# A four-block transformer kernel: the entries of its two narrow attentions reordered

## The reference

```python
x = x + _L0_xattn_ref(_layernorm(x), ctx_1024, ctx_1024, wq, bq, wk, bk, wv, bv, wo, bo)
# inside: q from the norm of x; k and v from the context
scores = einsum('bthd,bshd->bhts', q, k) / sqrt(8)
probs  = softmax(scores)
x = x + (einsum('bhts,bshd->bthd', probs, v) @ wo.T + bo)
```

## Time and profile before

| | |
|---|---|
| times of three runs | 816.60, 821.52 and 816.17 us, median 816.6 |
| profiled execution | 821.47 us, of which the span of the records is 819.8 us |
| PE | 719.1 us busy, 88% of the span |
| DVE | 517.8 us, 63% |
| ACT | 439.8 us, 54% |
| POOL | 373.7 us, 46% |
| mean granted PE clock | 0.927 |

### The profile page before, as it was taken

The page is one execution under the profiler, slowest core; times in us unless marked ns, Lnnn a source line. Parts: engine busy times, 40 slices in busy tenths (PEclk is TensorE's granted clock), DMA queues, the critical chain, the costliest instruction groups (busy, mean ns, idle before and its releaser), DMA issues. The chain is left out here.

```text
span 819.8 us, 14606 instructions
## 1 busy us (share of the span) xinstructions
PE 719.1 (88%) x4942; PEld 584.4 (71%) x4942; DVE 517.8 (63%) x1415; ACT 439.8 (54%) x1344; POOL 373.7 (46%) x375
## 2 busy tenths in 40 slices
PE   6986799999899999897679999788879999996775
PEld 3654699998688887775558788556658888884754
DVE  5797774445676666575646677758765566566554
ACT  3893334444577776563124777489734466653221
POOL 6663312112576644433112677485441488864001
PEclk9599799999999999998959999979989999998669
DMA  7000011110000000000003445000010322200000
GB/s 277 2 2 26 14 27 52 40 49 14 1 2 2 2 8 2 1 1 0 7 21 97 145 141 177 16 2 2 3 48 26 103 97 90 78 14 1 0 1 26
DMA packets 14277, 33.13 MB, mean 40 GB/s; under 512 B 1744, under 2 KB 5864, under 8 KB 13952
## 3 DMA queue, kind: packets, MB, share of 16 engines
q1 hardware_dynamic: 14208, 32.26, 12.0%
HBM read 31.63 MB, written 0.62 MB: 39 GB/s over the span
## 5 line engine op out<-in xcount | busy, mean ns | idle before, releaser
L1233 PE MATMUL banks<-input_hi,weights_in_lo 128*128 128x512 f32 x296 | 123.9, 418 | 18.4 <-PEq L1617 11.9
L1233 PE MATMUL banks<-input_lo,weights_in_hi 128*128 128x512 f32 x296 | 118.9, 402 | 0.0
L1233 PE MATMUL banks<-input_hi,weights_in_hi 128*128 128x512 f32 x296 | 118.6, 401 | 0.0
L1233 PEld LDWEIGHTS banks<-weights_out,hidden 128*128 128x128 f32 x864 | 105.6, 200 | 11.1 <-issue 8.1
L1233 PE MATMUL banks<-weights_out,hidden 128*128 128x128 f32 x864 | 106.9, 284 | 7.0 <-PEq L1561 6.3
L992 ACT ACTIVATE probabilities<-banks,neg_max 128x128 f32<-128x128 f32 x256 | 92.3, 479 | 17.5 <-DVE neg_max L1945 17.5
L1095 ACT ACTIVATE hidden<-banks,cols 128x512 f32<-128x512 f32 x80 | 54.1, 689 | 75.5 <-ACTq L1093 75.1
L703 POOL TENSOR_TENSOR rstd<-var_eps,neg_half 128x4 f32<-128x4 f32 x24 | 24.9, 1038 | 136.1 <-POOLq L702 115.2
L1233 PEld LDWEIGHTS banks<-input_hi,weights_in_lo 128*128 128x128 f32 x296 | 57.5, 194 | 32.4 <-issue 17.3
L992 ACT ACTIVATION_READ_ACCUMULATOR probabilities<-banks,neg_max 128x1 f32 x256 | 72.9, 319 | 0.0
L813 POOL TENSOR_TENSOR hidden<-hidden,scratch 128x512 f32<-128x512 f32 x48 | 62.0, 1291 | 19.4 <-ACT hidden L1114 16.8
(11 more groups left out here) (277 smaller groups left out, 1734.3 us busy)
## 6 DMA issues: line engine op xcount, KB each, us to landing
scratch<-cw_rows SPq DMA_DIRECT2D x19, 512.0 KB, 3.9
weights_out<-w_in SPq DMA_DIRECT2D x17, 256.0 KB, 2.8
weights_in<-w_in SPq DMA_DIRECT2D x8, 512.0 KB, 3.6
weights_in<-w_in SPq DMA_DIRECT2D x9, 256.0 KB, 3.0
weights_in<-w_in SPq DMA_DIRECT2D x16, 128.0 KB, 2.2
weights_out<-w_in SPq DMA_DIRECT2D x16, 128.0 KB, 2.1
wq<-w1q_in SPq DMA_DIRECT2D x1, 1024.0 KB, 4.9
wo<-w1o_in SPq DMA_DIRECT2D x1, 1024.0 KB, 7.0
```

Of the source, the lines that this page charges most:

```text
L1233: return pe.matmul(o, l, rh, start=start, stop=stop, **kw)
```

## The change

On the SP queue x is loaded in two halves: first half, square weights, context, second half, with a semaphore of its own for the second. The statistics of each half wait for their own load.

In the plain attention PE now has the order keys of half 0, transposes of half 0, keys of half 1, queries of half 0, values. The other transposes (`turn_rest`, into bank 7 and no longer bank 1) come in step 1, the second half's queries in step 2 (before: step 0). ACT copies the second half's transposes after unit 0's exponentials (`rest_state`), and DVE copies the values after the maxima of unit 1 (`first_values`) and the second half's queries after those of unit 2. ACT does one exponential of a 128x1 column before anything else.

In the pruned attention PE's keys, values and transposes of half 0 come ahead; DVE does the second sum, then the norm of half 0, the split of the keys, the statistics of half 1, and the queries. The norm of half 1 follows the maxima of unit 0 (`rest_norm`), its power on POOL follows the first batch's queries and keys; transposes, values and queries of half 1 are placed as in the plain attention. In both, `add_bias` on POOL now waits for the second half's queries.

```diff
 # SP
-            sp.dma_start(x[:, :, :], x_in).then_inc(x_loaded, 16)
+            first = SQS["wk1"][0]
+            sp.dma_start(x[:, 0:4, :], x_in[:, 0:4, :]).then_inc(x_loaded, 16)
+            sp.dma_start(sq[:, 0:first], sq_in[:, 0:first]).then_inc(sq_loaded, 16)
             sp.dma_start(ctxT[:, :], ctxT_in).then_inc(ctx_loaded, 16)
-            first = SQS["wk1"][0]
-            sp.dma_start(sq[:, 0:first], sq_in[:, 0:first]).then_inc(sq_loaded, 16)
+            sp.dma_start(x[:, 4:8, :], x_in[:, 4:8, :]).then_inc(x_rest_loaded, 16)
 # POOL, spread_queries_keys and add_bias
+                    if prune and n == 0:
+                        inverse_roots((1,))
...
+                    pool.wait_ge(queries_ready, 2 * prune + 2)
                     pool.tensor_tensor(x[:, :, :], x[:, :, :], row_b("bo2" if prune else "bo0"), ALU.add)\
 # ACT
+            def take_state(half):
+                act.wait_ge(transposed, 1)
+                act.sem_inc(transposed, -1)
+                act.activation(xnT[:, half * 512:(half + 1) * 512], bank[7 * half][:, :], ACT.Copy)\
+                    .then_inc(feat_ready, 1)
             def enter_narrow(prune):
...
+                round_keys(prune, 0)
+                if prune:
+                    round_keys(prune, 1)
+                take_state(0)
+                if not prune:
+                    round_keys(prune, 1)
...
-                    pipelined(act, [(exps, range(UNITS), 1)], UNITS, 1, st.close)
+                    pipelined(act, [(exps, range(UNITS), 1), (rest_state, (0,), 1)], UNITS, 1, st.close)
...
             act.wait_ge(cols_loaded, 16)
+            act.activation(gap_exp[:, 0:1], col("bq0"), ACT.Exp).then_inc(st.sem, st.one())
+            act.wait_ge(st.sem, st.n)
+            st.close()
 # PE, steps (the pruned list is changed alike)
-                    pipelined(pe, [(scores, range(UNITS), 0), (rest_queries, (0,), 0),
+                    pipelined(pe, [(scores, range(UNITS), 0), (turn_rest, (0,), 1), (rest_queries, (0,), 2),
                                    (values, range(1, UNITS, 2), 3), (turn, range(UNITS), 2),
 # PE, entries
-            project(w("wk0"), ctxT, 2, (0, 1), keys_projected)
-            transpose_tiles(xn)
+            project(w("wk0"), ctxT, 2, (0,), keys_projected)
+            transpose_half(0, xn, 0)
+            project(w("wk0"), ctxT, 2, (1,), keys_projected)
...
             project_tok(w("wv2"), ctxT, 4)
-            transpose_tiles(xn)
+            transpose_half(0, xn, 0)
 # DVE, steps of the pruned and of the plain attention
                     pipelined(dve, [(pad, (0,), 0), (inverse_sums, range(UNITS), 2), (maxima, range(UNITS), 0),
-                                    (rest_queries, (0,), 0), (copy_second, range(UNITS), 2),
+                                    (rest_norm, (0,), 0), (first_values, (0,), 1), (rest_queries, (0,), 2),
+                                    (copy_second, range(UNITS), 2),
...
-                                    (rest_queries, (0,), 0), (scale_out, range(1, UNITS, 2), 3),
+                                    (first_values, (0,), 1), (rest_queries, (0,), 2), (scale_out, range(1, UNITS, 2), 3),
 # DVE, entries
-            split_keys(False)
+            split_keys(False, 0)
+            split_keys(False, 1)
             copy_queries(False, 0)
-            copy_values(iv, 4, "bv0", values_copied)
...
-            for half in range(2):
-                add_sums(half)
-                norm_stats(half, x, 1e-5)
-            for half in range(2):
-                norm_apply(half, x, xn, norm_tok_ready)
-            split_keys(True)
-            copy_values(iv, 4, "bv2", values_copied)
+            add_sums(0)
+            norm_stats(0, x, 1e-5)
+            add_sums(1)
+            norm_apply(0, x, xn, norm_tok_ready)
+            split_keys(True, 0)
+            split_keys(True, 1)
+            norm_stats(1, x, 1e-5)
             copy_queries(True, 0)
```

More of the change, by code:

```diff
@@ L973, in enter_halves, with round_keys @@
                 return take
-            def enter_narrow(prune):
-                for half in range(2):
[L977 to L980, removed]
-                for half in range(2):
[L982 to L985, removed]
+            def round_keys(prune, half):
+                tokens = slice(half * 512, (half + 1) * 512)
+                act.wait_ge(keys_projected, 2 * prune + half + 1)
+                act.activation(in_hi[:, 0, tokens], bank[2 + half][:, :], ACT.Identity,
+                               bias=col("bk2" if prune else "bk0")).then_inc(keys_rounded, 1)
+            def take_state(half):
[3 more added lines that the diff above has]
+                    .then_inc(feat_ready, 1)
+            def enter_narrow(prune):
+                round_keys(prune, 0)
[4 more added lines that the diff above has]
+                    round_keys(prune, 1)
             def narrow_attention(prune):
@@ L1000, in copy_first, with rest_state @@
                         .then_inc(first_copied[prune], 1)
+                def rest_state(it, n):
+                    take_state(1)
                 if prune:
-                    pipelined(act, [(exps, range(UNITS), 1), (copy_first, range(UNITS), 2)], UNITS, 1, st.close)
+                    pipelined(act, [(exps, range(UNITS), 1), (rest_state, (0,), 1), (copy_first, range(UNITS), 2)],
+                              UNITS, 1, st.close)
                 else:
-                    pipelined(act, [(exps, range(UNITS), 1)], UNITS, 1, st.close)
+                    pipelined(act, [(exps, range(UNITS), 1), (rest_state, (0,), 1)], UNITS, 1, st.close)
             def round_heads():
@@ L1275, in narrow_attention, with turn_rest @@
             def narrow_attention(prune):
+                def turn_rest(it, n):
+                    transpose_half(1, xn, 7)
                 def rest_queries(it, n):
+                    pe.wait_ge(feat_ready, 1)
+                    pe.sem_inc(feat_ready, -1)
                     project(w("wq2" if prune else "wq0"), xnT, 6, (1,))
@@ L1891, in norm_x @@
                 for half in range(2):
+                    dve.wait_ge((x_loaded, x_rest_loaded)[half], 16)
                     norm_stats(half, x, 1e-5)
@@ L1904, in copy_queries @@
             def copy_queries(prune, half):
-                dve.wait_ge(projected, 1)
+                dve.wait_ge(projected, 3 if prune and half == 0 else 1)
                 dve.sem_inc(projected, -1)
@@ L1910, in copy_queries, with split_keys @@
                     .then_inc(queries_ready, 1)
[L1912 to L1919, removed]
+            def split_keys(prune, half):
+                tokens = slice(half * 512, (half + 1) * 512)
+                dve.wait_ge(keys_rounded, 2 * prune + half + 1)
+                dve.scalar_tensor_tensor(in_lo[:, 0, tokens], bank[2 + half][:, :],
+                                         col("bk2" if prune else "bk0"), in_hi[:, 0, tokens],
+                                         ALU.add, ALU.subtract).then_inc(keys_split, 1)
             def copy_values(dst, at, bias, done=None):
@@ L1946, in maxima, with rest_norm, first_values @@
                         .then_inc(neg_max_ready[prune], 1)
+                def rest_norm(it, n):
+                    norm_apply(1, x, xn, norm_tok_ready)
+                def first_values(it, n):
+                    copy_values(iv, 4, "bv2" if prune else "bv0", values_copied)
                 def rest_queries(it, n):
```

11 lines of the change are left out of this document (4 added, 7 removed).

## The result

| | before | after |
|---|---|---|
| median of 7 runs each, same comparison | 817.28 us (816.17 to 821.52) | 826.13 us (824.24 to 830.52) |
| ratio after / before | | 1.0107 [1.0084, 1.0131], +8.85 us |
| profiled execution / its span | 821.5 / 819.8 us | 830.5 / 828.8 us |
| plain attention ends (taken at the start of its first addition into x) | 72.84 | 77.00 (+4.16) |
| sums ahead of the pruned attention start | 521.18 | 525.02 (+3.84) |

The distance between the two profiled executions, 9.05 us, is about that of the medians, so their traces can be set side by side. 4.2 us arise in the plain attention, 3.5 in the pruned one, 1.7 behind it. The last is no effect of the change that could be told from chance: the code behind the pruned attention is the same everywhere and takes 215.8 to 218.0 us in the profiles of this document (216.0 before, 217.7 after).

What follows compares the result with a forecast made beforehand. DVE was taken as tighter in the plain attention, ACT's start as deciding the pruned one, PE's clock as third. Plain entry +1.6, plain steps +2.5 and the rest 0 gave +4.1 on median 816.6; predicted 820.5, range 813 to 826.5.

Steps and rivals of the forecast that it cites:

- rival A: Slow clock stretch comes every time, in plain steps 1 to 3: 824.8, with +1.3 in the pruned attention 826; chance 0.25.
- the forecast's own range: Whole kernel: 818 to 823.5 us, given a chance of 0.45.
- Loads: Start of kernel, loads and first norm: halving and reordering x costs nothing, bound 0 to +0.3 us.
- Table load: ACT at the start: pulling the 1.28 us table load ahead gains nothing, as ACT would have been free anyway.
- Plain entry: Plain attention's start: PE waits for the norm and works at half speed, first queries end later; +1.6 (+0.4 to +1.6).
- Plain steps: Plain attention, steps 0 to 4: DVE's order delays `turn` 0 and maxima 4, start 13.3 after scores 0; +2.5 (+0.6 to +2.5).
- DVE being the tighter engine: Plain attention running evenly, 3.11 us a unit: DVE tighter than ACT, so a late maximum delays all that follow it.
- Pruned entry: Pruned attention's start: first exponential 2.5 us earlier, then given back; taken at 0 (-1.7 to +1.3).
- the branch at half clock: Pruned entry: scores 2, queries and transposes in one half-speed chain, unit 3's exponentials at 47.1 for 545.9; +1.2, with a wait +1.3.
- Each sign that was named: Pruned attention: first exponential 2.5 us earlier against the block before, ACT idle 1 to 3 us ahead of the first `copy_first`.
- the reading of the median: Median 816.6 taken as an execution without the plain attention's slow stretch, which cost about 4.1 us; profiled execution 821.5.

Runs made afterwards that it cites:

- retimed kernel: Kernel before with pruned attention as changed, but its second half's norm, transposes, state copy, values and queries one place earlier: 815.8 us, ratio 0.9973.
- changed kernel with the old loads: The changed kernel with x loaded whole and in the old order on the SP queue: 825.2 us, ratio 1.0073 against before.
- key order alone: Kernel before with only the transposes of half 0 put between the two halves' keys in the plain entry, on PE and ACT: 818.4 us, ratio 1.0013.
- plain part alone: The whole change except the pruned attention, which stays as before: 823.3 us, ratio 1.0074 against before.
- after filled: Changed kernel plus unread extra PE matmuls ahead of the pruned scores 0 and of units 0 to 4's transposes: 824.1 us, ratio 1.0070 against before.
- steps alone: Kernel before with only the plain attention's second transposes, values' copy and second queries moved to steps 1 and 2: 822.7 us, ratio 1.0069.
- pruned part alone: Kernel before with only the pruned attention changed, on all engines: 817.2 us, ratio 1.0006.
- loads alone: Kernel before with only x loaded in halves and the new order on the SP queue: 819.2 us, ratio 1.0023.
- before, filled: Kernel before plus twelve unread PE matmuls: two ahead of pruned scores 0, one ahead of units 0 to 4's transposes in both attentions: 819.5 us, ratio 1.0011.
- with values as before: Kernel before with the pruned attention changed, but its values copied ahead of the first steps, right after the first queries: 819.7 us, ratio 1.0004.
- with the table load: The retimed kernel plus one early exponential first on ACT: 816.1 us, ratio 0.9988 against before.
- retimed, filled: The retimed kernel plus the same unread extra PE matmuls: 817.8 us, ratio 1.0000 against before.

## Why the prediction was right or wrong

The time lies in the range, and the sign was right, but it lies only 0.4 below the upper end, in a part that was added for rival A; the forecast's own range ended at 823.5. The likeliest value, 820.5, is 5.6 too low: an increase of 4.1 was worked out and 8.85 measured. 826.1 is what rival A gave, by a mechanism that the runs don't bear out. That the range holds it is in good part luck.

**Loads: the step that failed.** "Nothing (0 to +0.3)" measured +1.5 at scores 0 and +1.9 [0.4, 3.3] in the time. I took it that the same bytes ahead of the context and the cols land when they did. Before, keys waited for the last of x, context and square weights, at 6.43; now the context is that last one, at 7.57, and the second half of x (8.11 for "6.5 at the earliest") holds DVE in a norm that wanted both. Keys, which I had perhaps 0.6 earlier, start 1.1 later.

**Table load: right.** The retimed kernel is not faster with it.

**Plain entry: the mechanism right, the size +1.1 for +1.6.** The changed kernel with the old loads measures this term: the queries end at 14.09 for the 14.6 worked out at half speed and 13.03 before, and scores 0 start at 15.94 for 16.5 and 14.88. They do run at half speed, 1.79 for 1.10. That the key order alone came to 14.7 and 16.55 is a coincidence, since it has a second group of transposes ahead of the queries which the sum did not have. Loads and order together make +2.57, of which 1.5 are the loads'. The choice of half speed was right, and other kernels bear it out. Where PE stood 1.1 to 1.6 us ahead of its first transposes (after, plain part alone, key order alone, old loads, after filled), the first queries take 1.55 to 1.92 us; in all other kernels, where it ran on from the keys, 1.09 to 1.10.

**Plain steps: the chain right, its size mixed with the clock.** `turn` 0 waits for the queries' copy, and maxima 4 stand where DVE's order puts them: 3.1 later in the filled kernels for the predicted 2.5. The 14.06 for the predicted 13.3 holds second queries of 2.05 for 1.02, in the one stretch of that kernel at 0.69, and one of the extra matmuls, which keeps `turn` 0 until 27.39 when the copy is done at 26.87. Less the first it is 13.0, less both about 12.6, by my estimate, so that at full clock the term may be nearer 2 than 3. Without fillers, at half clock in both, it is 16.23 for 11.6 (14.88 to 26.5 before), +4.6, and of that and the entry 4.2 are left at maxima 8, since the half clock ends sooner (36 for 38.4). In the time the steps alone measured +5.6 [3.8, 7.4], more than twice the 2.5. The places of the values and of the second queries were not run apart. That nothing is made good behind unit 8 is as DVE being the tighter engine would have it, but it doesn't show that: ACT is the busier one there, 28.83 of 31.30 us for DVE's 27.34 in after.

**Pruned entry: right alone, too small in the whole kernel.** Taken at 0 between -1.7 and +1.3, measured +0.5 [-1.3, +2.3] alone. In the whole kernel's profile it is +3.5, outside the bounds: the branch at half clock was worked out up to unit 3 only, and the half clock lasts 23.9 us there. Each sign that was named is there: the first exponential 1.9 earlier (2.6 in the pruned part alone) for 2.5, ACT idle 2.59 ahead of the first copy for "1 to 3 us", maxima 3 later by 1.7 for 1.3. The gain is real, and the half-speed chain of scores 2, queries and transposes takes it back; the retimed kernel keeps part of it by taking the queries out of that chain.

**The clock: the reading of the median failed.** I took the median to be an execution without the plain slow stretch. Every profiled kernel without fillers has one, of 7 to 17 us, also the one of 812 us; it is in both kernels (17.1 us before, 13.7 after) and adds nothing between them. Executions of the kernel before do differ by some 5 us, but a stretch that varies by as much is the unchanged one between the attentions: some 443 us in five profiles, each with 37.5 us at half clock there, and 448 to 449 in six with 44 to 51. So the difference of 4.9 need not have said anything about the plain attention. Its price was near, 4.1 worked out and 3.45 taken away by the fillers. Rival A therefore gets its number without its cause. What did grow is the half-clock stretch in the pruned attention. Length from first sum to last addition, by the time at half clock in the attention's first 40 us, each from one profile:

| pruned code | kernel | half clock, us | length, us |
|---|---|---|---|
| old | before; plain part alone | 10.2 | 82.5; 82.4 |
| old | loads alone; key order alone | 13.7 | 82.6; 82.6 |
| old | steps alone | 20.5 | 84.7 |
| old | before, filled | 6.8 | 83.8 |
| new | after, filled | 6.8 | 83.3 |
| new | pruned part alone; with values as before | 17.1 | 83.8; 83.9 |
| new | after; with old loads | 23.9 | 86.0; 85.8 |
| retimed | retimed; with the table load | 10.2 | 81.2; 81.2 |
| retimed | retimed, filled | 10.2 | 83.7 |

With the same code the attention is 2 us longer where the half clock lasts longest, though 13.7 us cost no more than 10.2; the filled rows hold extra work and can't be compared with the others. I put the surplus of the whole change over the sum of its halves, 8.85 for 6.5, down to this. The surplus itself isn't shown: the intervals are 6.9 to 10.7 for the whole, 4.3 to 7.8 and -1.3 to 2.3 for the halves, and they overlap. That PE's gaps in the entry (2.21 ahead of scores 0, where it also waits ahead of the queries) bring it on is argued; why the same pruned code draws 17 us after one plain attention and 24 after another stays open.

So the account is: plain entry +2.6 (1.5 of it gone with the old loads), steps about +3, pruned +0.5, and a remainder of 2 to 3. The sum of the first three is 6.1, and 6.5 is what the two halves alone measured. The remainder is not measured. That it is the clock fits with the extra matmuls, which bring the distance from 8.85 down to 4.6 in the times, but only from 7.7 to 6.2 in the landmarks of the two attentions.

## What to carry to other kernels

A late step costs nothing only until the next one on the same engine waits for it: moving half of an entry into the first steps must end before the first consumer behind it would have started, and one place earlier was the difference between +0.5 and -2.2 us here. When a load is split to let its first part land sooner, ask which transfer the consumer waits for last, and whether that one moved back. When a landmark of one profile is taken for an effect, compare it with how far it moves between profiles of the same code, here up to 3.3 us. Price each stretch at the clock that its own rows show, in both kernels, before crediting a variant with escaping it.

## What the runs showed of the hardware

**A norm on DVE slows beside POOL.** The same four instructions of 128x128, SBUF to SBUF, take 1.11 us with POOL idle (528.72 in after), 1.45 at 537.67 in after, 1.88 in the pruned part alone and 2.73 in the retimed kernel (522.08). POOL worked on masks and queries for about 0.8, 1.5 and 2.5 us of these. In the pruned part alone the norm begins at 526.68 beside a mask of 526.41 to 527.45 and ends at 528.56, just 1.11 behind the mask's end. Its masks stay at 1.03 to 1.04, and maxima, which read PSUM, at 1.22 to 1.23. Not all that runs beside POOL slows: statistics beside a mask take 0.86 (531.30 in after), and a norm beside POOL's power of 128x4 takes 1.11 (8.23 in the earlier trace rows). The Trainium skill, "GPSIMD Engine Reference", section 1 "Specifications", says that the two engines share SBUF interfaces and contend when DVE runs in a mode with two ports or has two SBUF inputs. The rows agree that they contend and give the price, up to 1.6 us for a norm; in which mode the norm runs, no row shows. The forecast had the norm at 1.12 there.

**A full row of the granted clock isn't full speed at the start.** In after it reads 1.00 from 7.5 to 9.7 and from 12.0 to 15.7 us, while two 128x512 matmuls take 1.84 to 2.04 there and 1.10 at 531.53. The trace holds no record of the grant before 15.40 in after (11.15 in before, 13.83 with the old loads), and the view shows 1.00 where nothing is recorded. The matmuls take half-speed times until about the first record and full-speed times behind it: 1.79 for two at 12.30 with the old loads, 1.10 at 11.93 in before.

**Short full-width work held the clock.** One filler of 1.1 us ahead of each of five transpose groups turned 17 us of 0.50 into 1.00 in the plain attention of before; its end came 3.45 us earlier. In the changed kernel, with 3.4 us at half clock for 13.7, it came 0.85 earlier. In the pruned attention, where ACT is full, the fillers cost 1.2.
